# A six-stage fp32 kernel: both ends of the state-space stage rebuilt, and the cross-attention's bias row added once to X

## The reference

```python
def _L0_attn_ref(x, W_in, conv_w, conv_b, W_x, W_dt, b_dt, A_log, Dp, W_out):
    xc, z = jnp.split(x @ W_in.T, 2, axis=-1)            # d_inner = 512
    xc = causal_depthwise_conv(xc, conv_w) + conv_b       # 4 taps
    xc = jax.nn.silu(xc)
    delta, Bm, Cm = split(xc @ W_x.T)                     # 64, 16, 16
    delta = jax.nn.softplus(delta @ W_dt.T + b_dt)
    deltaA = jnp.exp(delta[..., None] * -jnp.exp(A_log))
    BX = delta[..., None] * Bm[:, :, None, :] * xc[..., None]
    _, hs = jax.lax.associative_scan(combine, (deltaA, BX), axis=1)
    y = jnp.einsum('bldn,bln->bld', hs, Cm) + Dp * xc
    return y * jax.nn.silu(z) @ W_out.T

def _L1_xattn_ref(src, tgt, mask, Wq, bq, Wk, bk, Wv, bv, Wo, bo):
    ...                                                   # 16 heads of 16
    attn = jax.nn.softmax(scores * D_QKV ** (-0.5), axis=-1)
    out = jnp.einsum('bhts,bhsk->bhtk', attn, v)
    return jnp.einsum('btd,ed->bte', out, Wo) + bo

x = x + _L0_attn_ref(_layernorm(x), ...)
x = x + _L0_ffn_ref(_layernorm(x), ...)
x = x + _L1_xattn_ref(ctx_1024, _layernorm(x), fside_SxS2_0, ...)
```

## Time and profile before

| | us |
|---|---|
| median of 3 runs | 2436.21 |
| the profiled execution | 2440.47 |
| its span | 2438.8 |
| state-space stage, start to first scan unit | 331.0 to 388.7 |
| its 128 scan units | 388.7 to 874.2 |
| last sums, output projection, additions | to 888.3 |
| experts of layer 0 | 888.3 to 1228.5 |
| cross-attention: queries, then batches | 1228.5 to 1260.9 to 1555.6 |

### The profile page before, as it was taken

One profiled execution on the slowest core, in us unless ns is written; L12 is line 12 of the kernel. 1 busy time (PEld: TensorE's weight loads), 2 busy tenths in 40 slices (PEclk: granted clock), 3 DMA queues, 4 the chain that ended last, 5 costly groups with the idle time before them and its releaser, 6 DMA issues. The chain is left out here.

```text
span 2438.8 us, 38889 instructions
## 1 busy us (share of the span) xinstructions
PE 1899.6 (78%) x11338; PEld 1316.8 (54%) x11339; DVE 1554.0 (64%) x3359; ACT 1027.3 (42%) x2932; POOL 1240.5 (51%) x999
## 2 busy tenths in 40 slices
PE   5699977988888667899768999699737999998000
PEld 5378852333333243577537888588513888877000
DVE  5499916999999969333436777477687333333733
ACT  1367727575757313233127777434206333332000
POOL 1388614676767620688405555366101555443775
PEclk9699988999999988999969999899665999999555
DMA  6311013030303024799611111000311899899332
GB/s 213 91 72 71 9 32 139 21 118 16 123 9 131 0 75 140 171 298 234 151 37 31 32 32 32 29 2 2 124 62 46 274 286 281 281 263 223 108 116 86
DMA packets 163804, 272.04 MB, mean 112 GB/s; under 512 B 28722, under 2 KB 97300, under 8 KB 162708
## 3 DMA queue, kind: packets, MB, share of 16 engines
q1 hardware_dynamic: 130708, 199.72, 24.9%
q0 software_dynamic: 30464, 68.19, 12.1%
q10 hardware_dynamic: 2496, 2.44, 0.4%
HBM read 218.74 MB, written 51.53 MB: 111 GB/s over the span
## 5 line engine op out<-in xcount | busy, mean ns | idle before, releaser
L981 POOL TENSOR_TENSOR b_h<-b_h,b_bcb 128x1024 f32<-128x1024 f32 x128 | 301.8, 2358 | 151.4 <-DVE b_h L1019 150.8
L1514 POOL DMA_INDIRECT m1x_xb<-scratch_xn,m_tok x192 | 182.9, 953 | 335.3 <-DVE m1x_yb L1643 174.9
L837 PE MATMUL b_psy<-b_h,ident 128*128 128x512 f32 x512 | 255.0, 625 | 75.3 <-POOL b_h L981 75.1
L1019 DVE TENSOR_TENSOR_SCAN b_h<-b_dA,b_pbx 128x1024 f32<-128x1024 f32 x128 | 292.6, 2286 | 4.4
L1561 PE MATMUL m1x_psh<-m1x_xe,m1x_w 128*128 128x128 f32 x1536 | 210.4, 280 | 20.6 <-DMA m1x_w<-in_m_w 17.9
L837 PEld LDWEIGHTS b_psy<-b_h,ident 128*128 128x128 f32 x512 | 94.6, 196 | 218.8 <-POOL b_h L981 130.2
L1561 PEld LDWEIGHTS m1x_psh<-m1x_xe,m1x_w 128*128 128x128 f32 x1536 | 189.0, 194 | 32.1 <-issue 20.6
L939 ACT ACTIVATE b_dA<-b_delta,b_A 128x504 f32<-128x504 f32 x256 | 166.8, 706 | 92.9 <-DVE b_h L1019 87.4
L1630 DVE TENSOR_TENSOR m1x_hT<-m1x_sg,m1x_psh 128x128 f32<-128x128 f32 x192 | 55.2, 288 | 234.4 <-ACT m1x_sg L1613 145.0
L1013 DVE TENSOR_TENSOR b_pbx<-b_pdx,b_bcb 128x1024 f32<-128x1024 f32 x128 | 157.6, 1231 | 51.1 <-ACT b_pdx L923 45.0
L1816 POOL TENSOR_TENSOR x_s<-x_s,x_rs 128x1024 f32<-128x1024 f32 x64 | 121.1, 1893 | 134.4 <-DVE x_rs L1983 134.3
(11 more groups left out here) (436 smaller groups left out, 4409.0 us busy)
## 6 DMA issues: line engine op xcount, KB each, us to landing
m1x_w<-in_m_w SPq DMA_DIRECT2D x192, 256.0 KB
b_bcb<-scratch_bc_rows SPq DMA_DIRECT2D x64, 512.0 KB, 4.8
scratch_y<-m1x_yb SPq DMA_DIRECT2D x192, 128.0 KB
m_w<-in_m_w SPq DMA_DIRECT2D x64, 368.0 KB
a_c<-in_ctxT SPq DMA_DIRECT2D x16, 512.0 KB, 3.7
...
```

The costliest lines, as they stand in the source:

```text
L837: mm = pe.matmul(psy[:, k % 2, :], ident[:, :], h[:, u % HB, j, :], start=False, stop=(nq == NQ - 1 and j == CQ - 1))
L981: q.tensor_tensor(hs, hs, bcb[:, 1, CQ * nq:CQ * nq + CQ], ALU.mult).then_inc(sem("hc"), 1)
L1019: v.tensor_tensor_scan(h[:, u % HB].rearrange("p j n -> p (j n)"), dA[:, u % DB].rearrange("p j n -> p (j n)"), pbx[:, :, :].rearrange("p ...
L1514: g.indirect_dma_start(out=xb[:, j, :], out_offset=None, in_=xn, in_offset=bass.IndirectOffsetOnAxis(ap=tok[:, b:b + 1], axis=0)).then_inc ...
```

## The change

Head of the stage. Three of the nine loads (win, convw, convb) get semaphores of their own. POOL clears the padding and a row of zeros at once, the decay tiles only after the norm's bias. ACT starts with the norm. In group 0, the convolutions of chunks 0 to 2 are done by DVE as a multiply-add chain of four taps straight into xc (convolved); chunk 3 stays on PE, and its four diagonals are the first ones made. ACT then applies Silu chunk by chunk (to chunks 0 to 2 from xc, to chunk 3 from PSUM), and takes the exponential of A behind it.

Tail of the stage. The last group's output projection goes chunk by chunk: last_output(c) runs behind unit 13, 21 and 29 of the last group and once more at the end. It accumulates all four tiles in the two banks of psw, which two products with a row of zeros have started. DVE makes the row statistics for the next stage: twelve tiles before the last gating, four after the last additions; the router's start loses them.

Cross-attention. In the query stage the bias row is spread over 128 partitions by one product with the row of ones, behind ACT's copy of it and ahead of the projections, and DVE adds it to all of X in four operations; the product per tile pair goes.

```diff
@@ -712,13 +712,14 @@
...
 ddiag = sb("ddiag", [P, NCH, P])
+zero = sb("zero", [1, P])
...
-LOADS = [(win[:, :, :], d["b_win"]), (convw[:, :, :], d["b_convw"]), (convb[:, :], d["b_convb"]),
-         (wx[:, :, :], d["b_wx"]), (wdt[:, :], d["b_wdt"]), (bdt[:, :], d["b_bdt"]),
+FIRST = [(win[:, :, :], d["b_win"], "win"), (convw[:, :, :], d["b_convw"], "convw"), (convb[:, :], d["b_convb"], "convb")]
+LOADS = [(wx[:, :, :], d["b_wx"]), (wdt[:, :], d["b_wdt"]), (bdt[:, :], d["b_bdt"]),
@@ -733,20 +734,22 @@
...
 DVE_AT = {"O": (71, 72, 74, 75)}
-YZ = 2
+YZ, LAST = 2, 5
...
+ONV = 3
...
-    first = [(at[r], n, r) for n, at in table.items() for r in range(len(at)) if at[r] < NU]
+    first = [(at[r], n, r) for n, at in table.items() for r in range(len(at)) if at[r] < NU and not (n == "V" and r < ONV)]
...
 turn = {}
-for piece in ahead(PE_AT) + [q for u in range(NU * NG) for q in due(PE_AT, u // NU, u % NU)] + [("O", NG - 1, t) for t in range(4)]:
+for piece in ahead(PE_AT) + [q for u in range(NU * NG) for q in due(PE_AT, u // NU, u % NU)]:
@@ -773,6 +776,8 @@
...
     def _(sp):
+        for dst, src, name in FIRST:
+            sp.dma_start(dst, src).then_inc(sem(name), 16)
@@ -797,19 +802,19 @@
...
                     taken(pe, "T", g, t)
-                pe.wait_ge(sem("weights"), W_ALL)
+                pe.wait_ge(sem("win"), 16)
...
                 taken(pe, "X", g, r)
-                pe.wait_ge(sem("pads"), 2)
-                pe.wait_ge(sem("cdiag"), NCH * KC)
+                pe.wait_ge(sem("cdiag"), NCH * KC if g else KC)
...
             elif name == "B":
-                pe.wait_ge(sem("silu"), g + 1)
+                pe.wait_ge(sem("weights"), W_ALL)
+                pe.wait_ge(sem("silu"), NCH + g)
@@ -838,6 +843,20 @@
...
+        def last_output(c):
+            pe.wait_ge(sem("yz"), NCH * (NG - 1) + c + 1)
+            if c == 0:
+                for t in (2, 3):
+                    taken(pe, "O", NG - 2, t)
+                pe.wait_ge(sem("zero"), 1)
+                for s in range(2):
+                    pe.matmul(psw[:, s, :], zero[:, :], bc(zero[:, None, :], [1, GT // P, P]), start=True, stop=False)
+            for t in range(4):
+                mm = pe.matmul(psw[:, t // 2, (t % 2) * D:(t % 2) * D + D], yz[:, c, t * P:(t + 1) * P], wout[:, c, :], start=False, stop=(c == NCH - 1 and t % 2 == 1))
+                if c == NCH - 1 and t % 2:
+                    mm.then_inc(sem("last"), 1)
@@ -845,16 +864,14 @@
...
                 summed(g, i)
-        for t in range(4):
-            piece("O", NG - 1, t)
+                if g == NG - 1 and i % NQ == LAST and i >= NQ:
+                    last_output(i // NQ - 1)
+        last_output(NCH - 1)
...
         ln.scalar_std(a)
-        a.wait_ge(sem("weights"), W_ALL)
-        a.activation(A[:, :, :], A[:, :, :], ACT.Exp).then_inc(sem("A_exp"), 1)
         a.wait_ge(sem("ln_bias"), 1)
-        a.wait_ge(sem("pads"), 2)
@@ -873,16 +890,32 @@
...
                 s = reader_takes(a, name, g, r)
-                if g or r >= 2:
+                a.wait_ge(sem("xcp_pad"), 1)
+                if g == 0 and r >= 2:
+                    a.wait_ge(sem("conv0"), r - 1)
+                elif g == 1 and r < 1:
+                    a.wait_ge(sem("conv0"), ONV)
+                elif g:
...
                              ).then_inc(sem("psw_free", s), 1)
+            elif name == "V" and g == 0:
+                a.wait_ge(sem("convb"), 16)
+                s = reader_takes(a, name, g, r)
+                for c in range(ONV):
+                    a.wait_ge(sem("conv0"), c + 1)
+                    a.activation(xc[:, 0, c, :], xc[:, 0, c, :], ACT.Silu).then_inc(sem("silu"), 1)
+                a.activation(xc[:, 0, r, :], psw[:, s, :], ACT.Silu, bias=convb[:, r:r + 1]).then_inc(sem("psw_free", s), 1)
+                a.wait_ge(sem("psw_free", s), bank(name, g, r)[1] + 1)
+                a.sem_inc(sem("silu"), 1)
+                a.wait_ge(sem("weights"), W_ALL)
+                a.activation(A[:, :, :], A[:, :, :], ACT.Exp).then_inc(sem("A_exp"), 1)
...
                 a.activation(xc[:, g % 2, r, :], psw[:, s, :], ACT.Identity, bias=convb[:, r:r + 1]).then_inc(sem("psw_free", s), 1)
-            elif name == "S":
+            elif name == "S" and g:
@@ -931,6 +964,7 @@
...
                 a.wait_ge(sem("A_neg"), 1)
+                a.wait_ge(sem("dA_pad"), 1)
@@ -951,8 +985,10 @@
...
     def _(q):
-        q.memset(dA[:, :, :, :], 0.0).then_inc(sem("pads"), 1)
-        q.memset(xcp[:, :, :, 0:KC - 1], 0.0).then_inc(sem("pads"), 1)
+        q.memset(xcp[:, :, :, 0:KC - 1], 0.0).then_inc(sem("xcp_pad"), 1)
+        q.memset(zero[:, :], 0.0).then_inc(sem("zero"), 1)
+        q.wait_ge(sem("ln_bias"), 1)
+        q.memset(dA[:, :, :, :], 0.0).then_inc(sem("dA_pad"), 1)
@@ -961,7 +997,7 @@
...
             q.wait_ge(sem("delta"), k + 1)
-            q.wait_ge(sem("silu"), g + 1)
+            q.wait_ge(sem("silu"), NCH + g)
@@ -992,15 +1028,34 @@
...
         ln.vector_bias(v)
-        v.wait_ge(sem("weights"), W_ALL)
-        for c in range(NCH):
+        v.wait_ge(sem("convw"), 16)
+        v.wait_ge(sem("convb"), 16)
+        def diagonals(c):
...
                 v.tensor_scalar(cdiag[:, c, k, :], ident[:, :], convw[:, c, k:k + 1], None, ALU.mult).then_inc(sem("cdiag"), 1)
+        def convolved(c):
+            out = xc[:, 0, c, :].rearrange("p (b l) -> p b l", b=NB)
+            taken(v, "X", 0, c)
+            v.tensor_scalar(out, xcp[:, c % 2, :, 0:S], convw[:, c, 0:1], convb[:, c:c + 1], ALU.mult, ALU.add).then_inc(sem("tap"), 1)
+            for k in range(1, KC):
+                v.wait_ge(sem("tap"), (KC - 1) * c + k)
+                v.scalar_tensor_tensor(out, xcp[:, c % 2, :, k:k + S], convw[:, c, k:k + 1], out, ALU.mult, ALU.add
+                                       ).then_inc(sem("tap" if k < KC - 1 else "conv0"), 1)
+        diagonals(NCH - 1)
+        for c in range(ONV):
+            convolved(c)
+        for c in range(NCH - 1):
+            diagonals(c)
+        v.wait_ge(sem("weights"), W_ALL)
...
         v.tensor_scalar(A[:, :, :], A[:, :, :], -1.0, None, ALU.mult).then_inc(sem("A_neg"), 1)
-        v.wait_ge(sem("pads"), 2)
+        v.wait_ge(sem("dA_pad"), 1)
@@ -1039,9 +1094,15 @@
...
                 scanned(g, i)
+        for t in range(4 * (NG - 1)):
+            v.bn_stats(e["stats"][:, t, :], X[:, t, :]).then_inc(sem("next_bn"), 1)
...
         for t in range(4):
-            added(NG - 1, t)
+            v.wait_ge(sem("last"), t // 2 + 1)
+            v.tensor_tensor(X[:, NT - 4 + t, :], X[:, NT - 4 + t, :], psw[:, t // 2, (t % 2) * D:(t % 2) * D + D], ALU.add).then_inc(sem("last_added"), 1)
+        for t in range(4):
+            v.wait_ge(sem("last_added"), t + 1)
+            v.bn_stats(e["stats"][:, NT - 4 + t, :], X[:, NT - 4 + t, :]).then_inc(sem("next_bn"), 1)
@@ -1358,8 +1419,6 @@
...
-            if capped:
-                ln.vector_tile_stats(v)
@@ -1735,6 +1794,7 @@
...
     pb = q.ps("pb", [1, D])
+    pbb = q.ps("pbb", [P, D])
@@ -1754,6 +1814,8 @@
...
                 pe.wait_ge(qs("xnT_ready", u), NT // 2)
+            pe.wait_ge(qs("bias_out"), 1)
+            pe.matmul(pbb[:, :], one[:, :], bias[:, :], start=True, stop=True).then_inc(qs("bias_rows"), 1)
@@ -1782,6 +1844,11 @@
...
                     ln.vector_tile(v, p, u)
+            v.wait_ge(qs("bias_rows"), 1)
+            for m in range(0, NT, GT // P):
+                x4 = X[:, m:m + GT // P, :]
+                v.tensor_tensor(x4, x4, bc(pbb[:, None, :], [P, GT // P, D]), ALU.add).then_inc(qs("x_biased"), 1)
+            v.wait_ge(qs("x_biased"), NT * P // GT)
@@ -1885,9 +1952,8 @@
...
             pe.wait_ge(sem("taken"), 2 * p + 2)
-            pe.matmul(psO[:, D:2 * D], one[:, :], bias[:, :], start=True, stop=False)
             for f in range(F2):
-                mm = pe.matmul(psO[:, D:2 * D], oT[:, p % 2, f, :], wo[:, f, :], start=False, stop=(f == F2 - 1))
+                mm = pe.matmul(psO[:, D:2 * D], oT[:, p % 2, f, :], wo[:, f, :], start=(f == 0), stop=(f == F2 - 1))
```

## The result

On the same chip, in alternation with the kernel before (2435.4 us median), the changed kernel takes 2416.3 us (2412.9 to 2418.4): a ratio of 0.9915, 95% interval 0.9893 to 0.9937. So the gain is about 21 us by the first and 25 us by the second, where the prediction's sum was 30.8. The profiled execution of after spans 2411.2 us.

A forecast was written before the change was run, and what follows sets the result against it. Bounds were read by stage: a chain of single steps in the state-space head, DVE in the scan, PE in the cross-attention loop. 19.5 + 5.2 + 6.1 = 30.8 us off 2440.5 gives 2409.7, forecast 2405 for the median; range 2397 to 2420.

The forecast's parts named there:

- the likeliest case: Whole kernel: the forecast of 2405 us with its unsure terms and scatter, spanning 2399 to 2411; 60%.
- (a): Rival, state-space head: PE's clock falls in its gaps (5.3 us less gain) or DVE's chain is dearer (5 less); 17%.
- tail, to the next stage's start: State-space stage's end: output projection and bn_stats moved earlier let the next stage start 3.4 us earlier.
- router beyond that: Next stage's start: the fifth normed tile, waiting for a store behind loads, reaches PE earlier; tail and router together 5.2 us.
- query stage: Cross-attention: an added product and PE's wait for ACT's copy cost 1.1 us, 2.4 at most.
- cross-attention's loop: Sixteen bias products leave PE, which stays the engine waited for: 16 x 0.45 = 7.2 us gained.
- steps 1 to 3: State-space head: earlier norm start, earlier X projection copy, three convolutions on DVE at about 2.8 us a chunk.
- Step 4: State-space head: four Silus, table load hidden in ACT's wait (else 1.3 us); projection at 355.3, 16.5 us gained so far.
- Step 5: State-space head: projection to dt, B and C keeps full clock, 3.6 us, 1.7 more gained (bounds +1.7 and -1.6).
- Step 6: State-space head: exponential of A behind Silu, hidden under PE, removes the later exponential table load; 1.3 us gained.
- (b): Rival, cross-attention's loop: the ring PE, DVE, ACT, POOL binds, so the loop's 7 us are not seen; 2412; 12%.
- (d): Rival, cross-attention's loop: PE loses its full clock for a part, making the kernel slower, 2482 for a third; 3%.

The follow-up runs named there:

- the second: The unaltered changed kernel measured again on another chip against the kernel before: ratio 0.9899 (0.9884 to 0.9913), 24.6 us less.
- load_first: Changed kernel plus a one-column Silu ahead of ACT's wait, moving only the table load; ran once, profile only: first scan unit after 39.9 us, not 42.2.
- tail alone: The kernel before with only the change's tail of the state-space stage: ratio 0.9997 (0.9987 to 1.0007).
- bias direct: Changed kernel with the query stage's bias made on all 128 rows at once, without ACT's copy and fourth product: ratio 0.9897 to the kernel before.
- all mended: Changed kernel with early Silus, 128-row bias, shared loads behind four stores, logits awaiting only gate weights, later small-table casts: ratio 0.9857 to the kernel before.

## Why the prediction was right or wrong

The time, 2416, lies in the range (2397 to 2420) and 11 us above the forecast of 2405. It lies beyond the 2399 to 2411 of the likeliest case, and the gain is about two thirds of the 30.8 forecast. Some 8 us of the 11 are terms of the sum, point by point; the other 3 are within the scatter of this one measurement, since the second gave 24.6 us. The range held because it was widened for rivals, of which the clock half of (a) came.

| term | forecast | measured |
|---|---|---|
| head | 19.5 | 15.4 |
| tail, to the next stage's start | 3.4 | 3.3 |
| router beyond that | 1.8 | 0.6 at the reduction, 0.3 at the stage's end |
| query stage | -1.1 | -2.7 |
| cross-attention's loop | 7.2 | 6.6 |
| sum | 30.8 | 22.9 |

The sum takes the router at the stage's end. That term is the first mixture stage's mean in the three profiles without the new tail (340.5) less that in the eight with it and with the loads in their old place (340.2); so small a difference is at the edge of what these profiles tell.

**Head, steps 1 to 3: right.** The norm starts 2.13 us after the stage's start (forecast 2.1). From there to the X copy it is 8.88 us (9.07). DVE's convolutions come every 2.82 us (2.8), so the near row of the scan unit, and not the 0.9 us idle of the earlier trace rows, was the one to take. The clearing on POOL delayed nothing.

**Step 4: wrong by 1.3 us.** The forecast put the table load into ACT's wait and named the other case at its price. It is the other case: the load is at 346.33, behind the wait. The projection started 15.2 us earlier than in before, relative to the stage, and not 16.5. load_first shows that the load moves into the wait if an instruction that needs it stands ahead of the wait. The load ends at 347.61 and the Silu starts at 347.62. The Trainium skill, ScalarE: Activation LUTs, section What ACT_TABLE_LOAD costs, adds a drain of about 1.38 us to every switch; none shows behind this load, and ahead of it the wait of 3.83 us could hide one. Where ACT does not wait the trace has none on either side:

```profile
359.54 0.63 ACT L943 ACTIVATE b_th<-b_th 128x512 f32<-128x512 f32 x1
360.18 1.28 ACT L945 ACT_TABLE_LOAD   x1
361.48 0.63 ACT L945 ACTIVATE b_th<-b_th 128x512 f32<-128x512 f32 x1
```

The measurement decides: the forecast was right to leave it out.

**Step 5: wrong by 2.7 us, and this is the largest miss.** The projection took 6.39 us: 1.0 more than in before, where 1.7 less was forecast. The step failed in its comparison. It took as precedent a scan unit in which PE works 2.0 of 3.6 us, so that it is never idle for more than 1.6 us at once, and applied it to gaps of 1.9 and 2.6. The first gap, 2.02 us, did keep the clock. The second, 3.75 with the load in it, did not; nor did 2.42 us when the load was taken out of it, which is just the gap that the forecast's own times give (352.9 to 355.3; it wrote 2.6). Nor is the gap's length all that counts. In the three profiles with the old head a longer gap, 4.08 us, made the same eight instructions take only 5.37 us; there PE had worked without a wait from 347.63 to 367.74. In the five with the new head and the Silus where after has them, 3.75 us made them 6.3 to 6.5, with 3.7 us of work ahead and 2.02 us of waiting before that. No run tells these two apart. Of rival (a) this is the half about the clock; the half about DVE's chain did not occur. It priced 3.6 us for a slow convolution, which did not come, and 1.7 for a projection as slow as before, which came and cost 1.0 more, inside the forecast's bound of 1.6. The Trainium skill, TensorE: Matmul & The Clock Gate, section HAM oscillation, cited there, tells of bursts that start cold after a wait. This row agrees: the burst behind 3.75 us ran at a granted clock of 0.57.

**Step 6: right.** No table load stands before the first decay, 1.3 us.

**Tail: right to 0.1 us**, with the parts as priced (bn_stats 3.99 for 4.0, the late products 1.99 for 1.8).

**Router: mis-sized.** What binds was named (the store behind the loads). The step that failed took the times of before over, shifted by 3.4 us, though the first store now goes out right behind the last load and no longer 3.2 us after it. Before, the fifth tile started 5.4 us after that load's issue; in after it is 6.5 us. The loads land later as well, the last of them 6.0 us after its issue and not 4.8:

```profile
m_ws<-in_m_ws SPq DMA_DIRECT2D x1, 384.0 KB, 6.0
```

PE takes the tile 11.2 us after the stage's start, forecast 10.0, before 11.8. The 0.6 that is left is still there at the reduction over the other eight tiles (33.9 us for 34.5) and at the first product of the routing (42.8 for 43.4), and nearly gone at the products that build the token lists, 74.1 and 73.9 us after the stage's start. These are before and after:

```profile
962.39 1.66 PE L1254 MATMUL m0r_psc<-m0r_atb,m0r_atp 128*128 128x64 f16 x8 [2.15 <-DVE m0r_atp L1425]
```

```profile
936.91 1.66 PE L1315 MATMUL m0r_psc<-m0r_atb,m0r_atp 128*128 128x64 f16 x8 [3.27 <-ACT m0r_atb L1348]
```

A product of the shared expert in between looks like the loss, again before and after:

```profile
944.67 3.67 PE L1098 MATMUL m0r_pst<-m_xnT,m_ws 128*128 128x512 f32 x8 [2.08 <-issue]
```

```profile
917.97 5.37 PE L1159 MATMUL m0r_pst<-m_xnT,m_ws 128*128 128x512 f32 x8 [2.07 <-issue]
```

It is not. The same product after the same gap took 3.67 us in nine of the fourteen profiles and 5.37 in five (both of after, tail alone, bias direct, all mended). In those five the clock had risen earlier among the short routing products ahead of it, which took 6.7 to 6.9 us from first to last and 7.4 to 8.1 in the nine. With the new tail and the loads in their old place the token lists' products start on average 74.0 us after the stage's start in the four profiles with the slow product and in the four with the fast one. So the 0.6 goes in that stretch either way, and what places the rise of the clock there no run tells.

**Cross-attention: half right.** PE was what the loop waits for, 211.6 busy of 213 us at a clock of 1.00, so rivals (b) and (d) did not occur. Two batches take 16.39 us instead of 16.80 (forecast 16.35), by the adds to X at both ends of thirteen pairs ((1500.83 - 1287.77) / 13 and (1529.87 - 1311.44) / 13): 0.41 for a forecast 0.45. The query stage cost 2.7 us, just beyond the bound of 2.4. Its projections start 1.8 us later and not 1.45, and then take 0.9 more on average, since fewer of them run at full clock (0.86 over the stretch, 0.95 in before), where I had expected 0.35 back. bias_direct takes back 2.5 of the 2.7.
